# Bringing the score maxima of a group into the queries' tile by two DMAs through memory instead of by TensorE and VectorE

## The chip, the cores and the metric

One core of one Trainium2 chip. The metric is the device time of one execution in microseconds (us). All times here are of that one core.

## What is computed

The input is x, 16 sequences ("quarters", q = 0 to 15) of 512 tokens with 256 features. Six residual blocks follow each other; the code names them by letters:

```python
x = x + 0.5 * _L0_ffn_ref(_layernorm(x), ...)     # A: coupling network, 3 cycles
x = x + _L0_attn_ref(_layernorm(x), ...)          # B: causal attention, 16 heads, latent keys, rope
x = x + 0.5 * _L0_ffn_ref(_layernorm(x), ...)     # C
x = x + 0.5 * _L1_ffn_ref(_layernorm(x), ...)     # D: small feature network
x = x + _L1_attn_ref(_layernorm(x), ...)          # E: attention with strided keys, then an MLP (E2)
x = x + 0.5 * _L1_ffn_ref(_layernorm(x), ...)     # F
```

What matters here is the softmax inside B and E:

```python
scores = jnp.einsum('bhqd,bhkd->bhqk', q, k) * scale
attn = jax.nn.softmax(scores, axis=-1)
```

Everything is float32. A row maximum is taken from the scores before the exponential.

## The kernel before

All weights stay in SBUF. The kernel is a software pipeline over the 16 sequences: `TURN` (L30) is a list of steps written out by hand, such as `1:max.B.1.2`, "for the sequence one turn ahead, stage B, group 1, round 2 of the maxima". `all_steps` (L101) unrolls it over the turns t; every engine walks the same list and runs its own part of each step, so each engine's queue is in this order and semaphores join them. Some 16 turns of about 215 us are in full swing, with a shorter opening and ending.

Attention works by groups of four heads (`GROUPS` = 4); head j of a group has the 32 partitions from 32j on, of which 16 hold the head's features. There are 4 groups for B and 4 for E in each sequence, 128 in all. A group goes through these steps:

- `content` (and `turn`, the rope part of B): queries and keys into tiles of `MAT`, and a copy in a faster format into `HI` by GpSimd.
- `max` (`maxima`, L636, on TensorE; `row_maxima`, L896, on VectorE): scores with the queries on the partitions, from `HI`, and their row maxima into `MX` (L208), which has the queries of one tile on the 128 partitions.
- `shift`: TensorE transposes `MX` (four 128x128 transposes, `turned`, L486, called at L784), so that the maxima lie along a row again, and `shifted` (L918) on VectorE subtracts the result from the whole queries' tile in `MAT`. `MX` is zero but in columns 16, 48, 80 and 112, so that only row 16 of each head's 32 rows changes: minus the maximum of each query. The keys' tile holds 1.0 in that row (`c_one`, through the bias at L1135, and through `c_qkb` for E, L1017), so that the product of queries and keys is the score less its maximum.
- `exp` (`exponents`, L665): the scores again, transposed and from `MAT`, one to four rounds for a group; round 0 begins with a wait for the shift (L668). ScalarE takes the exponentials into `PR` (L1174).
- `sum`, `divide`: the values weighted and divided.

In PSUM, banks 0 to 3 are used in pairs (`max`, `exp` and two more), bank 4 holds the sums, and banks 5 to 7 go round for all else, the shift included. TensorE works in order: when `exp` waits, all that stands behind it in the list waits too.

Round 0 of B's `exp` stands close behind the group's last `max` in the list: for group 0, between `max.B.0.2` and `exp.B.0.0` are `tf.C.1`, `divide.E.0`, `content.B.1`, `v.B`, `shift.B.0`, `att.E` and `mix.C.1`.

SyncE (SP) issues all DMAs. After the weights it walks over the sequences (L1361 to L1375): it waits until the last block F of a sequence has been added to `X`, stores it, waits until the store has landed and loads another sequence into the same place.

Of the kernel before, what the change touches and what calls it, by code (L numbers as in the profile page):

```python
# [7 lines left out]
F32 = mybir.dt.float32  # L8
# [6 lines left out]
P = 128  # L15
# [8 lines left out]
HALVES_OVER = [(n + RD // 2) % RD for n in range(RD)]  # L24
LN_EPS = 1e-5
# [6 lines left out]
0:mix.C.2.1 1:exp.B.0.2 -1:up.1 1:turn.B.2.q 1:max.B.1.2 -1:up.2 1:content.B.2 0:back.C -1:up.3 1:shift.B.1 -1:up.4  # L32
0:stats.D 1:exp.B.1.0 0:normal.D -1:up.5 -1:up.6 1:max.B.2.0 -1:bias.E2.0 0:xt.D -1:up.7 1:max.B.2.1 0:inner.D
0:relu.D.0 -1:down.0 1:max.B.2.2 -1:bias.E2.1 0:relu.D.1 0:relu.D.2 0:relu.D.3 0:bias.D.0 -1:down.1 1:sum.B.0.2
0:bias.D.1 -1:centre 1:exp.B.1.1 1:shift.B.2 1:sum.B.1.0 -1:scale 1:exp.B.1.2 -1:stats.F 1:sum.B.1.1 1:turn.B.3.k
-1:normal.F 1:exp.B.2.0 0:mout.D -1:xt.F -1:bias.F.0 0:stats.E 1:turn.B.3.q -1:inner.F -1:relu.F.0 1:divide.B.0
0:normal.E -1:relu.F.1 1:content.B.3 -1:relu.F.2 1:sum.B.1.2 -1:bias.F.1 1:exp.B.2.1 1:sum.B.2.0 -1:relu.F.3
1:exp.B.2.2 0:xt.E 1:max.B.3.0 0:content.E.3 0:bias.E.0 -1:mout.F 1:max.B.3.1 0:part.E.0 1:sum.B.2.1 1:max.B.3.2
0:part.E.1 1:divide.B.1 0:v.E 1:shift.B.3 0:max.E.3.0 1:sum.B.2.2 2:stats.A 2:normal.A 1:exp.B.3.0 0:content.E.2
1:exp.B.3.1 1:sum.B.3.0 2:xt.A 1:divide.B.2 1:exp.B.3.2 2:h1.A.0 0:content.E.1 2:h2.A.0 0:shift.E.3 0:max.E.2.0  # L40
2:h3.A.0 1:sum.B.3.1 1:sum.B.3.2 0:shift.E.2 2:tf.A.0 0:max.E.1.0 2:mix.A.0.0 0:content.E.0 0:bias.E.1 2:mix.A.0.1
2:h1.A.1 1:divide.B.3 0:max.E.1.1 2:h2.A.1 1:att.B 2:h3.A.1 0:exp.E.3.0 2:tf.A.1 2:mix.A.1.0 1:proj.B 2:mix.A.1.1
0:exp.E.2.0 1:stats.C 2:h1.A.2 0:sum.E.3.0 1:normal.C 2:h2.A.2 0:shift.E.1 1:xt.C 2:h3.A.2 0:max.E.0.0 0:divide.E.3
2:tf.A.2 2:mix.A.2.0 0:sum.E.2.0 2:mix.A.2.1 0:max.E.0.1 1:h1.C.0 2:back.A 0:exp.E.1.0 2:stats.B 0:divide.E.2
2:normal.B 1:h2.C.0 0:max.E.0.2 0:sum.E.1.0 1:h3.C.0 2:xt.B 1:tf.C.0 0:max.E.0.3 2:latent.B 0:shift.E.0 1:mix.C.0.0
0:exp.E.1.1 2:turn.B.0.k 0:exp.E.0.0 0:sum.E.1.1 2:kvt.B 2:turn.B.0.q 0:exp.E.0.1 0:sum.E.0.0 2:content.B.0
0:exp.E.0.2 0:exp.E.0.3 0:sum.E.0.1 1:mix.C.0.1 2:turn.B.1.k 1:h1.C.1 2:max.B.0.0 2:turn.B.1.q 1:h2.C.1 0:divide.E.1
2:max.B.0.1 0:sum.E.0.2 0:sum.E.0.3 1:h3.C.1 2:max.B.0.2 1:tf.C.1 0:divide.E.0 2:content.B.1 2:v.B 2:shift.B.0
# [66 lines left out]
def build(nc, ins, out):  # L115
# [14 lines left out]
    with ctx:  # L130
# [51 lines left out]
        c_one, c_ones = col(), col(4)  # L182
# [25 lines left out]
        MX = sb("MX", [P, TT, P])  # L208
# [107 lines left out]
        with nc.Block() as block:  # L316
# [81 lines left out]
            def _(pool):  # L398
# [5 lines left out]
                pool.affine_select(out=c_ones, in_=c_ones, compare_op=ALU.not_equal, fill=1.0, base=-HD,  # L404
# [43 lines left out]
        with nc.Block() as block:  # L448

            @block.tensor  # L450
            def _(pe):
# [297 lines left out]
                for name, *a in STEPS:  # L749
# [64 lines left out]
            def _(dve):  # L814
# [211 lines left out]
                for name, *a in STEPS:  # L1026
# [20 lines left out]
                    elif name == "shift":  # L1047
                        shifted(*a)
# [364 lines left out]
```

## Time and profile before

| | us |
|---|---|
| median of 3 runs | 3690.88 |
| lowest and highest | 3689.16, 3691.62 |
| span of the profiled execution, first to last instruction | 3688.1 |

The page of the profile gives the span of the profiled execution and no total of its own; the median of the runs is 2.8 us above that span. Of the span, TensorE's matmuls are busy 3457.0 us (94%), VectorE 2271.7 us (62%), ScalarE 1887.2 us (51%), GpSimd 955.1 us (26%). The program moves data over its DMA queues almost only in the first 50 us; afterwards there is one store and one load of 512 KB in each turn.

How to read it: PE is TensorE, PEld its weight loads, DVE VectorE, ACT ScalarE, POOL GpSimd, SP SyncE; SPq marks instructions by which SP issues a DMA. A row of the timeline has start in us, duration in us, engine, line, operation, output <- input, and xN, the number of instructions that it merges.

### The profile page before, as it was taken

How to read it: one execution, taken by the hardware profiler on the slowest of the kernel's cores; microseconds unless marked ns; L12 is line 12 of the kernel's file. 1: busy time of each engine (PE TensorE's matmuls, PEld its weight loads, DVE VectorE, ACT ScalarE, POOL GpSimd, SP SyncE). 2: the span in 40 equal slices, each digit the busy share in tenths (PEclk: the TensorE clock that was granted, in tenths of full speed). 3: DMA queues.
4: the chain of work that ended last, by engine and by line, in shares of the span. 5: the costliest groups of instructions: out<-in, count | busy, mean ns of one | idle time of the engine just before them, and what ended most of it. 6: DMA issues, size and time to landing. Idle time of an engine off the chain costs nothing.

```text
span 3688.1 us, 63212 instructions
## 1 busy us (share of the span) xinstructions
PE 3457.0 (94%) x24928; PEld 2002.6 (54%) x24928; DVE 2271.7 (62%) x4778; ACT 1887.2 (51%) x2919; POOL 955.1 (26%) x1069
## 2 busy tenths in 40 slices
PE   4789999999999999999999999999999999999876
PEld 3355556565555656555555655555565555555443
DVE  3446576666756666675666667566666756676442
ACT  2234655546465564646556464555646555564422
POOL 2213132331313232131222323122231313223111
PEclk8798999999999999999999999999999999999977
DMA  3000000000000000000000000000000000000000
GB/s 92 1 1 1 1 1 12 1 13 1 13 1 1 13 1 13 1 13 1 1 12 1 13 1 8 5 1 13 1 13 1 1 13 1 12 1 7 1 6 6
DMA packets 40882, 27.73 MB, mean 8 GB/s; under 512 B 19600, under 2 KB 39696, under 8 KB 40592
## 3 DMA queue, kind: packets, MB, share of 16 engines
q1 hardware_dynamic: 40592, 23.69, 2.2%
q8 instruction: 203, 3.33, 0.4%
q14 instruction: 87, 0.71, 0.1%
HBM read 15.30 MB, written 8.39 MB: 6 GB/s over the span
## 4 chain that ended last, share of the span: by engine, by line
PE 82%; DVE 12%; ACT 3%; issue 2%; POOL 0%; DVEq 0%; ACTq 0%; POOLq 0%
PE ps L478 74%; PE ps L489 8%; DVE MX L915 2%; DVE XN L843 1%; ACT other L1200 1%; DVE MX L909 1%; DVE XN L894 1%; DVE XN L891 1%; DVE XT L854 1%; DVE LT L881 1%; DVE XN L892 1%; DVE XT L853 1%; ACT PR L1174 0%; DVE stats L834 0%; DVE other L851 0%
## 5 line engine op out<-in xcount | busy, mean ns | idle before, releaser
L1174 ACT ACTIVATE PR<-ps 128x1024 f32<-128x1024 f32 (+3 forms) x592 | 524.5, 931 | 341.9 <-PE ps L478 340.6
L478 PE MATMUL ps<-MAT 32*128 32x512 f32 (+5 forms) x4928 | 593.3, 503 | 14.4 <-DVE MX L909 4.4
L915 DVE TENSOR_REDUCE MX<-ps 128x2 f32<-128x1024 f32 (+3 forms) x512 | 391.8, 818 | 203.7 <-PE ps L478 201.4
L1246 POOL TENSOR_TENSOR rstd<-var,neg_half 128x4 f32<-128x4 f32 x144 | 148.7, 1033 | 1311.3 <-DVE var L826 1183.5
L478 PEld LDWEIGHTS ps<-MAT 32*128 32x128 f32 (+2 forms) x4928 | 290.4, 199 | 262.4 <-issue 162.7
L478 PE MATMUL ps<-XT,cn_w 128*128 128x256 f32 x1536 | 367.6, 390 | 13.5 <-DVE XT L853 8.5
L478 PEld LDWEIGHTS ps<-XT,cn_w 128*128 128x128 f32 x1536 | 290.5, 193 | 99.7 <-issue 28.7
L478 PE MATMUL ps<-other,cn_w 128*128 128x512 f32 (+2 forms) x1152 | 321.0, 480 | 16.1 <-ACT other L1082 5.4
L921 DVE SCALAR_TENSOR_TENSOR MAT<-ps,MAT 128x512 f32<-128x512 f32 x128 | 88.5, 691 | 300.9 <-PE ps L489 300.3
L1281 POOL TENSOR_TENSOR MAT<-XN 128x512 f32<-128x512 f32 x128 | 167.3, 1307 | 402.4 <-DVE XN L894 241.8
L1304 POOL TENSOR_SCALAR_AFFINE_SELECT PR<-PR 128x512 f32<-128x512 f32 (+1 forms) x192 | 158.8, 827 | 410.0 <-ACT PR L1174 409.8
L909 DVE TENSOR_REDUCE MX<-ps 128x2 f32<-128x1024 f32 (+6 forms) x256 | 220.0, 902 | 59.6 <-PE ps L478 58.8
L1295 POOL CAST HI<-MAT 128x512 fp32r<-128x512 f32 (+3 forms) x256 | 146.4, 585 | 388.2 <-ACT MAT L1141 248.4
L478 PE MATMUL ps<-XT,w_up 128*128 128x512 f32 x512 | 245.7, 611 | 0.9 <-ACT XT L1073 0.9
L478 PE MATMUL ps<-HI 32*128 32x256 f32 (+4 forms) x3072 | 209.2, 360 | 36.4 <-DVE MX L915 25.4
L1082 ACT ACTIVATE other<-ps,cols 128x512 f32<-128x512 f32 x192 | 121.4, 683 | 228.3 <-PE ps L478 228.3
L478 PE MATMUL ps<-w_down,other 128*128 128x256 f32 x1024 | 227.4, 380 | 0.0
L843 DVE TENSOR_SCALAR XN<-X,mv,rstd 128x256 f32<-128x256 f32 x384 | 183.6, 540 | 67.6 <-POOL rstd L1246 67.0
L1200 ACT ACTIVATE other<-ps,cols 128x512 f32<-128x512 f32 x256 | 179.2, 795 | 71.4 <-PE ps L478 71.4
L478 PEld LDWEIGHTS ps<-HI 32*128 32x128 f32 x3072 | 117.3, 192 | 176.3 <-issue 136.5
L478 PEld LDWEIGHTS ps<-w_down,other 128*128 128x128 f32 x1024 | 193.4, 190 | 33.9 <-issue 7.7
L1183 ACT ACTIVATE AO<-ps 128x512 f32<-128x512 f32 x128 | 77.0, 602 | 255.5 <-PE ps L478 255.3
(158 smaller groups left out, 5718.2 us busy)
## 6 DMA issues: line engine op xcount, KB each, us to landing
X<-in_L_attn_x SPq DMA_DIRECT2D x16, 512.0 KB, 3.9
out<-X SPq DMA_DIRECT2D x16, 512.0 KB, 3.0
w_up<-in_L_attn_W SPq DMA_DIRECT2D x1, 1024.0 KB, 6.8
w_down<-in_L_attn_W SPq DMA_DIRECT2D x1, 1024.0 KB, 8.8
w_krope<-in_L_attn_W_krope SPq DMA_DIRECT2D x1, 512.0 KB, 4.4
w_qk<-in_L_attn_Wqkv SPq DMA_DIRECT2D x4, 128.0 KB, 4.4
cn_w<-in_L_ffn_cn_w SPq DMA_DIRECT2D x1, 256.0 KB, 4.2
w_qrope<-in_L_attn_W_qrope SPq DMA_DIRECT2D x1, 256.0 KB, 3.1
```

The source lines that it names most:

```text
L478: return pe.matmul(dst, lhsT, rhs, start=start, stop=stop, skip_group_check=True)
L489: last = pe.transpose(dst[:, t * P:(t + 1) * P], src(t), ident[:])
L843: last = dve.tensor_scalar(XN[:, c, t, :], src[:, t, :], mv[:, c, t, 0:1], rstd[:, c, t:t + 1], ALU.subtract, ALU.mult)
L909: last = dve.tensor_reduce(MX[:, t0:t0 + len(parts), at], src[:, :, 0:len(parts) * nk].rearrange("p j (t k) -> p t j k", k=nk), AX_X, ALU.max)
L915: last = dve.tensor_reduce(MX[:, t, at], src[:, :, a:a + nk[pair]], AX_X, ALU.max)
L1082: freed(act.activation(H1[:, area_of[s], m, :], src, ACT.Gelu, bias=c_b1[:, m:m + 1]), "h1", s, q, k, m)
L1174: freed(act.activation(PR[0:m, tile_of((s, q, g, r)), 2 * pair:2 * pair + 2, lo:T], ps[0:m, b:b + 2, 0:T - lo], ACT.Exp, scale=SCALE[s]), ...
L1200: last = act.activation(U[:, area_of[s], j, :], src, ACT.Relu, scale=c_mw1[:, j:j + 1], bias=c_mb1[:, j:j + 1])
L1246: pool.tensor_tensor(rstd[:, c, :], var[:, c, :], neg_half[:], ALU.pow).then_inc(rstd_ready.sem, 1)
L1281: pool.tensor_tensor(dst, a, b, ALU.add).then_inc(rope_sum.sem, 1)
L1295: pool.tensor_copy(HI[:, content_tile((s, q, g), w, hi=True), 0:n], MAT[:, content_tile((s, q, g), w), 0:n]).then_inc(hi_ready.sem, 1)
L1304: pool.affine_select(out=p, in_=p, compare_op=ALU.is_ge, fill=0.0, base=0, pattern=[[0, 4], [0, n], [1, P]], channel_multiplier=-1).then_i ...
```

## The change

`shift` is no longer a step of the list: all `shift` tokens are taken out of `TURN`, and the order of all others stays. `MX` becomes four buffers (`SHIFTS` = 4) of 4 heads x 4 tiles for each partition, and needs no zeros around it. As soon as VectorE is through with the last `max` of a group, SP writes the 128 x 16 maxima to a scratch tensor in memory, element by element in the transposed order (each element is 4 bytes, and neighbours in the source lie 512 bytes apart in the destination), waits until they have landed, and reads them back as four rows of 512 into partitions 16, 48, 80 and 112 of the queries' tile in `MAT`. The row now holds plus the maximum, and the keys' row -1.0 in place of 1.0 (`c_less`). Round 0 of `exp` waits for the landing of the second transfer. SP's loop over the sequences is put into the order of the list, with the transfers among the stores and loads.

```diff
+SHIFTS = 4
-        MX = sb("MX", [P, TT, P])
+        MX = sb("MX", [P, SHIFTS, 4, TT])
+        maxima_d = nc.dram_tensor("maxima_d", (SHIFTS, 4, T), F32, kind="Internal").ap()
...
                 def exponents(s, q, g, r):
                     if r == 0:
-                        read_out(pe, "shift", s, q, g)
+                        n = number[s, q, g]
+                        pe.wait_ge(shift_landed[n % SHIFTS], 16 * (n // SHIFTS + 1))
...
-                    elif name == "shift":
-                        read_out(pe, *last_max(*a))
-                        turned(single_bank(), ("shift", *a), lambda t: MX[:, t, :])
...
                 def row_maxima(s, q, g, m):
-                    if m == 0 and n:
-                        when_full(dve, "shift", *GROUPS_DONE[n - 1])
+                    if m == 0 and n >= SHIFTS:
+                        dve.wait_ge(shift_landed[n % SHIFTS], 16 * (n // SHIFTS))
...
-                def shifted(s, q, g):
-                    src = when_full(dve, "shift", s, q, g)
-                    queries = MAT[:, content_tile((s, q, g), "q"), :]
-                    freed(dve.scalar_tensor_tensor(queries, src, -1.0, queries, ALU.mult, ALU.add), "shift", s, q, g)
...
+                def shifted(s, q, g):
+                    n = number[s, q, g]
+                    read_out(sp, *last_max(s, q, g))
+                    row, at = HD, n % SHIFTS
+                    sp.dma_start(maxima_d[at].rearrange("j (t p) -> p (j t)", p=P), MX[:, at, :, :],
+                                 allow_slow_non_contiguous=True).then_inc(maxima_out[at], 16)
+                    sp.wait_ge(maxima_out[at], 16 * (n // SHIFTS + 1))
+                    sp.dma_start(MAT[row:P:ROWS, content_tile((s, q, g), "q"), :], maxima_d[at]).then_inc(shift_landed[at], 16)
+
+                loaded_next(2)
+                for name, *a in STEPS:
+                    if name == "mout" and a[0] == "F":
+                        stored(a[1])
+                    elif name == "max" and a[3] == last_max(*a[0:3])[4]:
+                        shifted(*a[0:3])
```

## Rows read from the trace of the kernel before

**Rows 1.** The page: busy time, granted clock in 40 slices, chain.

```profile
PE 3457.0 (94%) x24928; PEld 2002.6 (54%) x24928; DVE 2271.7 (62%) x4778; ACT 1887.2 (51%) x2919; POOL 955.1 (26%) x1069
...
PEclk8798999999999999999999999999999999999977
...
PE 82%; DVE 12%; ACT 3%; issue 2%; POOL 0%; DVEq 0%; ACTq 0%; POOLq 0%
```

**Rows 2.** Groups by form: busy us, mean ns, idle before, of the shift.

```profile
L921 DVE SCALAR_TENSOR_TENSOR MAT<-ps,MAT 128x512 f32<-128x512 f32 x128 | 88.5, 691 | 300.9 <-PE ps L489 300.3
...
L489 PE MATMUL ps<-ident,MX 128*128 128x128 f32 x512 | 84.4, 290 | 7.7 <-DVE MX L909 6.4 <-DVE MX L915 1.2
```

**Rows 3.** Timeline, B's group 0: DVE's last maxima, then PE's shift to exp.

```profile
1549.30 1.95 DVE L915 TENSOR_REDUCE MX<-ps 128x2 f32<-128x256 f32 x4 [1.19 <-PE ps L478]
...
1553.08 0.66 PE L489 MATMUL ps<-ident,MX 128*128 128x128 f32 x4
1553.57 1.04 PE L489 MATMUL ps<-ident,ATN 128*128 128x128 f32 x8
1554.59 2.02 PE L478 MATMUL ps<-MAT 32*128 32x512 f32 x16
```

**Rows 4.** Timeline, last maxima and first exp of E0, B1, B2, B3.

```profile
1516.10 1.82 DVE L909 TENSOR_REDUCE MX<-ps 128x2 f32<-128x1024 f32 x2 [1.12 <-PE ps L478]
1523.10 1.26 PE L478 MATMUL ps<-MAT 32*128 32x512 f32 x8
...
1582.91 1.94 DVE L915 TENSOR_REDUCE MX<-ps 128x2 f32<-128x256 f32 x4
1590.14 2.01 PE L478 MATMUL ps<-MAT 32*128 32x512 f32 x16
...
1610.51 1.93 DVE L915 TENSOR_REDUCE MX<-ps 128x2 f32<-128x256 f32 x4
1625.58 2.01 PE L478 MATMUL ps<-MAT 32*128 32x512 f32 x16
...
1654.56 1.95 DVE L915 TENSOR_REDUCE MX<-ps 128x2 f32<-128x256 f32 x4 [1.68 <-PE ps L478]
1660.24 2.92 PE L478 MATMUL ps<-MAT 32*128 32x512 f32 x16
```

**Rows 5.** DMA issues: output<-input, count, KB each, median us to landing.

```profile
w_qdec<-in_L_attn_W_qdec SPq DMA_DIRECT2D x1, 128.0 KB, 4.4
...
cols<-in_L_attn_b SPq DMA_DIRECT2D x1, 4.0 KB, 2.4
...
cols<-in_L_ffn_W SPq DMA_DIRECT2D x4, 2.0 KB, 2.3
...
cols<-in_L_attn_beta SPq DMA_DIRECT2D x1, 1.0 KB, 2.1
...
rows<-in_L_attn_bout SPq DMA_DIRECT2D x1, 128.0 KB, 8.7
```

**Rows 6.** Timeline, VectorE's last addition of F and SP's store and load.

```profile
1649.69 1.28 DVE L967 TENSOR_TENSOR X<-ps,X 128x512 f32<-128x512 f32 x2
...
1651.04 0.38 SPq L1366 DMA_DIRECT2D out<-X  x1
1654.71 0.37 SPq L1368 DMA_DIRECT2D X<-in_L_attn_x  x1
```

**Rows 7.** Timeline of PE: an idle time in full swing; one product, opening and later.

```profile
1526.92 0.44 PE L570 MATMUL ps<-ident,LT 128*128 128x128 f32 x2 [1.59 <-DVE LT L881]
...
49.97 5.93 PE L478 MATMUL ps<-XT,cn_w 128*128 128x256 f32 x16 [2.66 <-DVE XT L853]
...
1560.09 3.62 PE L478 MATMUL ps<-XT,cn_w 128*128 128x256 f32 x16
```

**Rows 8.** Windows: length, busy times (x), then granted clock, DMA share, GB/s.

```profile
47.60:54.50 6.90, 4.54 (x11) 3.64 (x12) 2.95 (x8) 1.55 (x4) 0.00 (x0) 0.51 0.84 131
...
1658.70:1662.10 3.40, 3.40 (x32) 1.46 (x32) 3.21 (x12) 0.60 (x1) 0.04 (x1) 0.50 0.00 0
1662.10:1873.80 211.70, 207.01 (x1521) 120.57 (x1514) 138.43 (x285) 117.28 (x179) 58.85 (x65) 1.00 0.02 5
```

More of the change, by code:

```diff
@@ L31 @@
 1:turn.B.2.k 0:h2.C.2 -1:xt.E2 1:max.B.1.0 0:h3.C.2 1:sum.B.0.0 1:sum.B.0.1 0:tf.C.2 1:max.B.1.1 0:mix.C.2.0 -1:up.0
[L32 to L45, printed above, removed]
@@ L46 @@
-0:exp.E.1.1 2:turn.B.0.k 0:exp.E.0.0 0:sum.E.1.1 2:kvt.B 2:turn.B.0.q 0:exp.E.0.1 0:sum.E.0.0 2:content.B.0
-0:exp.E.0.2 0:exp.E.0.3 0:sum.E.0.1 1:mix.C.0.1 2:turn.B.1.k 1:h1.C.1 2:max.B.0.0 2:turn.B.1.q 1:h2.C.1 0:divide.E.1
-2:max.B.0.1 0:sum.E.0.2 0:sum.E.0.3 1:h3.C.1 2:max.B.0.2 1:tf.C.1 0:divide.E.0 2:content.B.1 2:v.B 2:shift.B.0
+0:mix.C.2.1 1:exp.B.0.2 -1:up.1 1:turn.B.2.q 1:max.B.1.2 -1:up.2 1:content.B.2 0:back.C -1:up.3 -1:up.4 0:stats.D
+1:exp.B.1.0 0:normal.D -1:up.5 -1:up.6 1:max.B.2.0 -1:bias.E2.0 0:xt.D -1:up.7 1:max.B.2.1 0:inner.D 0:relu.D.0
@@ new lines @@
+-1:down.0 1:max.B.2.2 -1:bias.E2.1 0:relu.D.1 0:relu.D.2 0:relu.D.3 0:bias.D.0 -1:down.1 1:sum.B.0.2 0:bias.D.1
+-1:centre 1:exp.B.1.1 1:sum.B.1.0 -1:scale 1:exp.B.1.2 -1:stats.F 1:sum.B.1.1 1:turn.B.3.k -1:normal.F 1:exp.B.2.0
+0:mout.D -1:xt.F -1:bias.F.0 0:stats.E 1:turn.B.3.q -1:inner.F -1:relu.F.0 1:divide.B.0 0:normal.E -1:relu.F.1
+1:content.B.3 -1:relu.F.2 1:sum.B.1.2 -1:bias.F.1 1:exp.B.2.1 1:sum.B.2.0 -1:relu.F.3 1:exp.B.2.2 0:xt.E 1:max.B.3.0
+0:content.E.3 0:bias.E.0 -1:mout.F 1:max.B.3.1 0:part.E.0 1:sum.B.2.1 1:max.B.3.2 0:part.E.1 1:divide.B.1 0:v.E
@@ new lines @@
+0:max.E.3.0 1:sum.B.2.2 2:stats.A 2:normal.A 1:exp.B.3.0 0:content.E.2 1:exp.B.3.1 1:sum.B.3.0 2:xt.A 1:divide.B.2
+1:exp.B.3.2 2:h1.A.0 0:content.E.1 2:h2.A.0 0:max.E.2.0 2:h3.A.0 1:sum.B.3.1 1:sum.B.3.2 2:tf.A.0 0:max.E.1.0
+2:mix.A.0.0 0:content.E.0 0:bias.E.1 2:mix.A.0.1 2:h1.A.1 1:divide.B.3 0:max.E.1.1 2:h2.A.1 1:att.B 2:h3.A.1
+0:exp.E.3.0 2:tf.A.1 2:mix.A.1.0 1:proj.B 2:mix.A.1.1 0:exp.E.2.0 1:stats.C 2:h1.A.2 0:sum.E.3.0 1:normal.C 2:h2.A.2
+1:xt.C 2:h3.A.2 0:max.E.0.0 0:divide.E.3 2:tf.A.2 2:mix.A.2.0 0:sum.E.2.0 2:mix.A.2.1 0:max.E.0.1 1:h1.C.0 2:back.A
@@ L49 @@
+0:exp.E.1.0 2:stats.B 0:divide.E.2 2:normal.B 1:h2.C.0 0:max.E.0.2 0:sum.E.1.0 1:h3.C.0 2:xt.B 1:tf.C.0 0:max.E.0.3
+2:latent.B 1:mix.C.0.0 0:exp.E.1.1 2:turn.B.0.k 0:exp.E.0.0 0:sum.E.1.1 2:kvt.B 2:turn.B.0.q 0:exp.E.0.1 0:sum.E.0.0
+2:content.B.0 0:exp.E.0.2 0:exp.E.0.3 0:sum.E.0.1 1:mix.C.0.1 2:turn.B.1.k 1:h1.C.1 2:max.B.0.0 2:turn.B.1.q 1:h2.C.1
+0:divide.E.1 2:max.B.0.1 0:sum.E.0.2 0:sum.E.0.3 1:h3.C.1 2:max.B.0.2 1:tf.C.1 0:divide.E.0 2:content.B.1 2:v.B
 0:att.E 1:mix.C.1.0 1:mix.C.1.1 2:exp.B.0.0 0:proj.E 0:stats.E2 1:h1.C.2 0:normal.E2 2:exp.B.0.1
@@ L224, in build @@
         const_pool, const_dve = sem("const_pool"), sem("const_dve")
-        PREPARED_FIRST, PREPARED_ALL, POOL_DONE = 14, 22, 25
+        PREPARED_FIRST, PREPARED_ALL, POOL_DONE = 14, 22, 24
         x_loaded = [sem(f"x_loaded{c}") for c in range(CH)]
         x_stored = [sem(f"x_stored{c}") for c in range(CH)]
+        shift_landed = [sem(f"shift_landed{n}") for n in range(SHIFTS)]
+        maxima_out = [sem(f"maxima_out{n}") for n in range(SHIFTS)]
+        maxima_d = nc.dram_tensor("maxima_d", (SHIFTS, 4, T), F32, kind="Internal").ap()
         full = [sem(f"bank_full{b}") for b in range(8)]
@@ L1360, in _, with loaded_next, stored @@
                     sp.dma_start(dst, src, allow_slow_non_contiguous=True).then_inc(loaded, 16)
-                for q in range(2, N):
-                    c = q % CH
-                    if q >= CH:
-                        for n in range(2):
-                            read_out(sp, "mout", "F", q - CH, n)
-                        sp.dma_start(o_v[q - CH], X[:, c]).then_inc(x_stored[c], 16)
-                        sp.wait_ge(x_stored[c], 16 * (q // CH))
-                    sp.dma_start(X[:, c], x_v[q]).then_inc(x_loaded[c], 16)
-                for q in range(N - CH, N):
+                def loaded_next(q):
+                    sp.dma_start(X[:, q % CH], x_v[q]).then_inc(x_loaded[q % CH], 16)
+                def stored(q):
                     c = q % CH
```

24 lines of the change are left out of this document (12 added, 12 removed).

## The prediction

> **What bounds the kernel now.** I read the page first: its busy times, the granted clock by slices and the chain that ended last. TensorE is busy 94% of the span, the slices in the middle hold their clock, and the chain is TensorE for 82% [rows 1]. The windows say it more sharply: in one turn in full swing TensorE is busy 207.0 of 211.7 us at the full clock [rows 8]. So the kernel is a queue of TensorE work. What is taken from that queue is gained; VectorE (62%) and ScalarE (51%) have room. And what makes the queue wait is lost nearly whole, since there are only some 4.7 us of idle time in a turn into which a wait could fall.
>
> Next I read the groups by form for what is removed [rows 2], then, for the one new wait, the timeline around the last maxima of each kind of group and its first `exp` [rows 3, 4]. The reader should look there at one number: the time from the end of VectorE's last reduction to TensorE's first product from `MAT`. That is the time in which the two transfers must be done. The DMA issues with their landings [rows 5] and SP's own queue [rows 6] price the transfers.
>
> **What is removed.** The subtraction: 128 x 0.691 us = 88.5 us of VectorE [rows 2]. It isn't what TensorE's queue waits for most of the time, so I count nothing for it; what hides it is VectorE's own idle time, and the wait of `exp` for it is replaced below. The transposes: 512 on TensorE. One lasts 290 ns in the mean, but they are pipelined; four of them hold the queue from 1553.08 to 1553.57, 0.5 us [rows 3]. There are 8 groups in a turn and 16 sequences: 128 x 0.5 = **64 us gained**. That is the whole gain that I can point to. Banks 5 to 7 are asked for once less in a group; no wait in the rows read hangs on them, so zero, with a few us either way in the range.
>
> **What is added: the path of the maxima.** After VectorE's last reduction of a group the path is: SP sees the semaphore; it issues the write of 2048 single elements; these land; SP issues the read back; that lands; TensorE goes on. No row shows such a transfer, so I go by the nearest.
> - SP's reaction: VectorE ends at 1650.97 and SP's store stands at 1651.04 [rows 6], 0.07 us; twice, 0.15 us.
> - The write. From below, `cols` of 4.0 KB is 1024 pieces of 4 bytes and landed 2.4 us after its issue; from above, the slowest 128 KB of the trace landed after 8.7 us [rows 5], though it waited behind two loads of 1 MB. Nearest in the number of pieces is `w_qdec`: 128 partitions with 16 runs each are 2048 pieces, of 64 bytes; it landed after 4.4 us [rows 5]. I take **4.4 us**, since the number of pieces, not their bytes, is what the two have in common. It may be less (it stood behind other small pieces) or more (all these rows write to SBUF and mine writes 4-byte pieces to memory).
> - The read back: four rows of 2 KB. Small loads land after 2.1 to 2.4 us [rows 5]; I take 2.3.
>
> Sum: 4.4 + 2.3 + 0.15 = 6.85, say **7.0 us** with the last semaphore; 4.85 from below (2.4 + 2.3 + 0.15), 11.25 from above (8.7 + 2.4 + 0.15).
>
> The Trainium skill (page "DMA: Bandwidth & Descriptors", section "Anatomy of one DMA") gives a DMA about 2.0 us fixed plus its bytes over 436 GB/s, measured for another issuing path. The rows agree with the fixed part for small loads (2.1 us) and not for 128 KB in 2048 pieces (4.4 us). By that rule the estimate for the two would be some 4.2 us, and the time that of the first rival below. The same page ("Rules for kernel authors") speaks against the change: a strided last dimension becomes one descriptor for each element, and a transpose by a rearranged access pattern is to be avoided. No run here shows such a write yet; that rule stands beside the second rival.
>
> **How much time the path has now.** From the end of the last reduction to the first `exp`:
> - B0: 1551.25 to 1554.59, 3.3 us [rows 3].
> - E0: 1517.92 to 1523.10, 5.2 us; B1: 1584.85 to 1590.14, 5.3 us; B3: 1656.51 to 1660.24, 3.7 us [rows 4].
> - B2: 1612.44 to 1625.58, 13.1 us [rows 4]; E1, E2 and E3, read in the same way, have more than that. These four are hidden at any price up to 13 us.
>
> Without the transposes that lie in it, each of these is 0.5 us shorter. The new idle time of TensorE is 7.0 less what is left: B0 4.2, B1 2.2, B3 3.8, E0 2.3. Together 12.5 us in a turn, x 16 = **200 us lost**. What is queued behind the waiting `exp` is everything: projections, coupling networks, the MLP. ScalarE, VectorE and GpSimd run dry with it, and none can give work back since TensorE is the bound.
>
> One wait that is there now goes away in exchange: behind E0's first `exp` TensorE is idle for 1.59 us at 1526.92 until VectorE has scaled `LT` [rows 7]; VectorE gets there without the `exp`, so a stop of 2.3 us just before it swallows it: 1.6 x 16 = **26 us back**.
>
> **The clock.** TensorE's clock doesn't come through long waits. In the opening, an idle time of 2.66 us goes with half clock (0.51 in that window [rows 8], the lower of the two levels, 1.2 GHz), and the 16 products behind it took 5.93 us where they take 3.62 us at the full clock [rows 7]: 2.3 us more. In full swing the idle time of 1.59 us goes without a loss. The clock has little to spare even now: it falls once in the turn, for 3.4 us, with TensorE busy all the time but on products of 32 rows [rows 8], and B3's first `exp` took 2.92 us there where B1's took 2.01 [rows 4]. So for B0 and B3 (4 us idle) I count 2.3 us each, for B1 and E0 (2.2 us, between the two cases) half of it: 2 x 2.3 + 2 x 1.15 = 6.9 us in a turn, x 16 = **110 us lost**.
>
> **SP's queue.** Each group puts two issues and a wait of 4 to 5 us on SP. SP also has the store and the load of a sequence; at 1651.04 it stores and at 1654.71 it loads [rows 6], and B3's maxima come at 1656.51, after both, so SP is free. The load has a queue in common with the maxima and may hold them up for a part of its flight; at most 2 us in 13 turns, 26 us, in the range only. E3's maxima come 3.5 us after B3's and wait for SP some 1 us, covered by over 30 us. VectorE's new wait before it writes `MX` is for the group four before and long fulfilled.
>
> **Sum.** -64 + 200 - 26 + 110 = +220 us. Span 3688.1 + 220 = 3908; the 2.8 us between span and median added, **3910 us**, 6% slower.
>
> **Rivals.**
> 1. *Both transfers at the smallest landing: faster.* 2.1 + 2.1 + 0.15 = 4.35 us. Then B0 waits 1.5 us and B3 1.1 us, the others not, no wait is long enough for the clock, and 2.6 x 16 = 42 us stand against the 64: 3669 us. For it: every small load lands so soon, and 8 KB is small [rows 5]. Against it: 2048 pieces, and the one row with as many took 4.4. It decides from below about 4.8 us for the path; at 4.85 without a loss of clock the sum is 3686 us, no change. 12 in 100: 7 faster, 5 the same.
> 2. *Scattered 4-byte writes are slow.* The path takes 11.25 us: waits of 8.4, 6.5, 8.0 and 6.6 us, less the 1.6, are 27.9 x 16 = 446; the clock falls four times in a turn, 4 x 2.3 x 16 = 147; with the 64 gained, +529: 4220 us. For it: no row has a write of small pieces to memory. Against it: in the rows pieces cost little. 20 in 100, of which a third beyond 4220.
> 3. *The waits as forecast, but the clock holds.* +110: 3801 us. For it: in full swing TensorE is busy before and behind each stop, unlike in the opening. Against it: the clock falls now without any stop. 18 in 100.
> 4. The forecast, with a path of 5.5 to 9 us and a loss of clock: 50 in 100.
>
> **How the numbers follow.** The forecast's own bounds are the path from 5.5 to 9 us. The range has to leave out no more than 2 in 10: from below the path at 4.85 us, with the half charge of the clock for B0 and B3 (-64 + 59 + 37 = +32), 3723, rounded to 3720; above, rival 2 at 4220. Left out are most of rival 1 and the slowest third of rival 2. A measurement of this kernel tells about 0.2%, 7 us, from no change. Slower by more than that holds in rivals 2 and 3 and the forecast, 0.88; faster 0.07; the same 0.05.
>
> **What would show it.** In the profile after: landings for the two new issues (4.4 and 2.3 us); TensorE idle before the first `MAT` product of B0 and B3 by about 4 us, of B1 and E0 by about 2 us, and of the other four by nothing; TensorE's busy time in a turn down by 4 us; slices of the granted clock below full in the middle of the run, with falls behind B0's and B3's stops; the idle time before `LT` gone. I'm wrong if the write lands under 2.5 us, if it lands over 8, or if the clock stays up.

## The result and the profile after

The changed kernel takes 4282.9 us in the median where the one before takes 3690.65 in the same comparison: a ratio of 1.160 (95% interval 1.1585 to 1.1618), 16% slower. The direction was forecast, the size was not: 3910 us was predicted, and the time lies above the range (3720 to 4220).

From the page of the profile after, the lines that answer to [rows 1]: busy times, granted clock in 40 slices, and the chain that ended last, by engine and by line.

```profile
span 4279.2 us, 62140 instructions
...
PE 3518.6 (82%) x24416; PEld 1984.2 (46%) x24416; DVE 2207.9 (52%) x4650; ACT 1886.1 (44%) x2919; POOL 964.8 (23%) x1068
...
PEclk8788999989989998999899999989999998999877
...
PE 63%; DMA 19%; DVE 13%; ACT 3%; issue 2%; POOL 0%; DVEq 0%; ACTq 0%; SPq 0%; POOLq 0%
PE ps L481 58%; DMA maxima_d<-MX 16%; PE ps L492 4%; DVE MX L916 4%; DMA MAT<-maxima_d 3%; DVE MX L910 1%; DVE XN L844 1%; ACT other L1194 1%; DVE XN L895 1%; DVE XN L892 1%; DVE XT L855 1%; DVE XN L893 1%; DVE XT L854 1%; DVE stats L835 0%; DVE other L852 0%
```

Three things stand in these lines. The DMAs, absent from the chain before, are 19% of it, and 16 of the 19 are the write of the maxima, 3 the read back. TensorE works less of the time (82% for 94%) but is busy 62 us longer, although 512 transposes are gone. And the slices of the granted clock that were full all through the middle now have 8s among them.

The DMA issues (KB each, median us from issue to landing; the landing of the last line is not given) and, from the list of waits (total us, times, longest), those of TensorE for the transfer and for `LT`:

```profile
maxima_d<-MX SPq DMA_DIRECT2D x128, 8.0 KB, 10.3
MAT<-maxima_d SPq DMA_DIRECT2D x128, 8.0 KB
...
PE ps L481 <- DMA MAT<-maxima_d: 559.4, 69, 12.6
...
PE ps L573 <- DVE LT L882: 7.4, 2, 3.7
```

The write lands after **10.3 us**; the prediction had 4.4. The timeline at B's group 0 of one turn shows the whole path; it answers to [rows 3]. VectorE's last maxima, SP's two issues, TensorE before and behind its wait:

```profile
2063.18 1.95 DVE L916 TENSOR_REDUCE MX<-ps 128x2 f32<-128x256 f32 x4 [1.19 <-PE ps L481]
...
2065.16 0.36 SPq L1369 DMA_DIRECT2D maxima_d<-MX  x1
2075.16 0.50 SPq L1372 DMA_DIRECT2D MAT<-maxima_d  x1
...
2066.95 1.09 PE L492 MATMUL ps<-ident,ATN 128*128 128x128 f32 x8
2077.02 3.81 PE L481 MATMUL ps<-MAT 32*128 32x512 f32 x16 [8.97 <-DMA MAT<-maxima_d]
```

The reduction ends at 2065.13; SP answers 0.03 us later, issues the read back 10.0 us after the write, and TensorE goes on 1.9 us after that: 11.9 us for a path that had 3.3. TensorE stands still for 8.97 us, and the 16 products behind the wait take 3.81 us where the same 16 took 2.02 in [rows 3].

The same turn has three more such waits, of E0, B1 and B3:

```profile
2036.95 2.11 PE L481 MATMUL ps<-MAT 32*128 32x512 f32 x8 [7.05 <-DMA MAT<-maxima_d]
...
2121.30 3.81 PE L481 MATMUL ps<-MAT 32*128 32x512 f32 x16 [6.89 <-DMA MAT<-maxima_d]
...
2202.70 3.81 PE L481 MATMUL ps<-MAT 32*128 32x512 f32 x16 [9.10 <-DMA MAT<-maxima_d]
```

Together with B0 that is 32.0 us in the turn. B2, E1, E2 and E3 wait for nothing there, as forecast.

Windows over B0's transfer (columns as in [rows 8]; the last three are granted clock, DMA share, GB/s) show what the chip did in that time:

```profile
2065.20:2068.50 3.30, 2.85 (x21) 1.93 (x20) 3.20 (x8) 3.13 (x5) 2.05 (x4) 1.00 0.31 7
2068.50:2071.00 2.50, 0.00 (x0) 0.00 (x0) 0.99 (x3) 2.03 (x3) 0.00 (x0) 1.00 0.00 0
2071.50:2076.00 4.50, 0.00 (x0) 0.00 (x0) 0.00 (x0) 0.00 (x0) 0.00 (x0) 0.50 0.00 0
2077.00:2081.50 4.50, 4.48 (x18) 1.92 (x19) 0.00 (x0) 0.65 (x1) 0.00 (x0) 0.50 0.00 0
```

The DMA engines have records of work only in the first 3.3 us after the issue of the write; the other 6.7 us until the landing pass with a DMA share of 0.00. And the granted clock falls to half while TensorE stands still, and is still at half when its products start again.

### The profile page after: what moved, and what is told of

Its sections match the earlier page's. It is cut to its first block, busy times and chain, and to the rows that moved or that the text cites. A ratio compares the mean times of both kernels' runs of the same rounds, so it can differ in the third digit from the quotient of the medians.

```text
span 4279.2 us, 62140 instructions
## 1 busy us (share of the span) xinstructions
PE 3518.6 (82%) x24416; PEld 1984.2 (46%) x24416; DVE 2207.9 (52%) x4650; ACT 1886.1 (44%) x2919; POOL 964.8 (23%) x1068
## 4 chain that ended last, share of the span: by engine, by line
PE 63%; DMA 19%; DVE 13%; ACT 3%; issue 2%; POOL 0%; DVEq 0%; ACTq 0%; SPq 0%; POOLq 0%
PE ps L481 58%; DMA maxima_d<-MX 16%; PE ps L492 4%; DVE MX L916 4%; DMA MAT<-maxima_d 3%; DVE MX L910 1%; DVE XN L844 1%; ACT other L1194 1%; DVE XN L895 1%; DVE XN L892 1%; DVE XT L855 1%; DVE XN L893 1%; DVE XT L854 1%; DVE stats L835 0%; DVE other L852 0%
## 5 line engine op out<-in xcount | busy, mean ns | idle before, releaser
L481 PE MATMUL ps<-MAT 32*128 32x512 f32 (+5 forms) x4928 | 676.0, 577 | 569.7 <-DMA MAT<-maxima_d 559.4
L481 PEld LDWEIGHTS ps<-MAT 32*128 32x128 f32 (+2 forms) x4928 | 308.8, 217 | 859.1 <-DMA MAT<-maxima_d 618.5
L892 DVE TENSOR_TENSOR XN<-ps,rope_sin 128x512 f32<-128x512 f32 x128 | 88.3, 690 | 330.4 <-PE ps L481 330.4
L921 DVE RECIPROCAL rden<-ps 128x16 f32<-128x16 f32 x128 | 32.3, 252 | 337.4 <-PE ps L492 336.9
## 6 DMA issues: line engine op xcount, KB each, us to landing
maxima_d<-MX SPq DMA_DIRECT2D x128, 8.0 KB, 10.3
```

The source lines that it names most:

```text
L481: return pe.matmul(dst, lhsT, rhs, start=start, stop=stop, skip_group_check=True)
L892: dve.tensor_tensor(b, src, rope_sin[:], ALU.mult).then_inc(rope_sines.sem, 1)
```

## The experiments

The waits of TensorE, the landings of the transfers and the clock were measured on kernels in which the way of the maxima differs. First the write. In most of these kernels the read back changes with it, so the landing of the write (the median of the 128 transfers of one execution) is what counts; their total times are of a single execution each. The later kernels, those with a ratio, ran four or five times.

### A contiguous write, the transposition moved to the read

```diff
-        maxima_d = nc.dram_tensor("maxima_d", (SHIFTS, 4, T), F32, kind="Internal").ap()
+        maxima_d = nc.dram_tensor("maxima_d", (SHIFTS, P, 4 * TT), F32, kind="Internal").ap()
-  sp.dma_start(maxima_d[at].rearrange("j (t p) -> p (j t)", p=P), MX[:, at, :, :], ...)
+  sp.dma_start(maxima_d[at], MX[:, at, :, :].rearrange("p j t -> p (j t)"))
-  sp.dma_start(MAT[row:P:ROWS, ..., :], maxima_d[at])
+  sp.dma_start(MAT[row:P:ROWS, ..., :].rearrange("j (t p) -> j t p", p=P), maxima_d[at].rearrange("p (j t) -> j t p", j=4), ...)
```

> The scratch tensor is laid out as the maxima lie in SBUF, so the write is 128 pieces of 64 bytes and the read back gathers 2048 pieces of 4 bytes; same values, the transposition only moves from the write to the read. In the changed kernel the write landed 10.3 us after its issue and the read back let TensorE go on 1.9 us after its own. Theory 1 (writing 2048 pieces of 4 bytes into memory is what is slow; reading as many is not): the write lands after 2.1 to 2.5 us; the read, on four destination rows, after 2 to 6 us; path 4.5 to 8.5 us, time 3720 to 4040 us. Theory 2 (2048 pieces are slow in whichever direction): write 2.3, read about 10 us, path 12.3, time about 4280 us as now. Theory 3 (any write of maxima to memory takes 10 us until it is confirmed): write stays at about 10 us, time 4280 us or more.

Measured: 3991.8 us, beside 3696.9 for the kernel before. The write's landing, and the same group of the timeline:

```profile
maxima_d<-MX SPq DMA_DIRECT2D x128, 8.0 KB, 1.4
...
1917.57 1.95 DVE L916 TENSOR_REDUCE MX<-ps 128x2 f32<-128x256 f32 x4 [1.20 <-PE ps L481]
...
1919.55 0.32 SPq L1369 DMA_DIRECT2D maxima_d<-MX  x1
1920.95 0.52 SPq L1371 DMA_DIRECT2D MAT<-maxima_d  x1
...
1928.10 2.96 PE L481 MATMUL ps<-MAT 32*128 32x512 f32 x11 [5.66 <-DMA MAT<-maxima_d]
```

A write of 128 pieces lands after 1.4 us, less than any load of [rows 5]; theory 3 is out. The read of 2048 pieces of 4 bytes, into four partitions, takes 7.2 us here until TensorE goes on (6.9 in the median of the groups that wait): dearer than theory 1 allowed, cheaper than theory 2 said. The path is 8.6 us in place of 11.9, and 290 us of the loss are gone. So scattering the write costs 8.9 us more than writing straight (10.3 less 1.4), and gathering the read some 5 us more than reading straight (6.9 less 1.9).

### Pieces of 16 bytes

The scratch tensor is laid out as heads x queries of a tile x tiles; the write has 512 pieces, of which four share 64 bytes, and the read goes by four transfers.

```diff
+        maxima_d = nc.dram_tensor("maxima_d", (SHIFTS, 4, P, TT), F32, kind="Internal").ap()
+  sp.dma_start(maxima_d[at].rearrange("j p t -> p j t"), MX[:, at, :, :], ...)
+  for j in range(4):
+      sp.dma_start(<row j of MAT>, maxima_d[at, j:j + 1].rearrange("o p t -> o t p"), ...)
```

> The scratch tensor as heads x queries of a tile x tiles: the write is 512 pieces of 16 bytes in place of 2048 of 4 bytes, the read back gathers pieces of 4 bytes by four transfers, one a head. Theory 1a (each small piece costs its time at the memory): the landing of the write falls in proportion to the pieces, 2.3 + 8.0 x (512 - 128)/(2048 - 128) = 3.9 us. Theory 1b (a fixed wait until scattered writes are confirmed, whatever their number): it stays near 10 us. The read back then takes 2.5 to 4 us; with 1a the path is 6.5 to 8 us and the time 3850 to 4000 us.

Measured: the write lands after 2.7 us, even sooner than in proportion to the pieces (3.9). A fixed wait for scattered writes (theory 1b) is out. The whole was no faster, 4312.7 us, and far from the 3850 to 4000 expected: the four gathering reads took what the write gave, with 593 us of waits of TensorE in all. In one group SP needs 6.05 us only to issue them, and in the median TensorE goes on 10.1 us after the first issue, not 2.5 to 4.

```profile
maxima_d<-MX SPq DMA_DIRECT2D x128, 8.0 KB, 2.7
...
2004.06 6.05 SPq L1374 DMA_DIRECT2D MAT<-maxima_d  x4
...
PE ps L481 <- DMA MAT<-maxima_d: 593.3, 74, 12.5
```

### As many pieces, but each with 64 bytes of its own

```diff
+        maxima_d = nc.dram_tensor("maxima_d", (SHIFTS, 4, T, 16), F32, kind="Internal").ap()
+  sp.dma_start(maxima_d[at, :, :, 0].rearrange("j (t p) -> p j t", p=P), MX[:, at, :, :], ...)
```

> Again 2048 pieces of 4 bytes into memory, but each into 64 bytes of its own (the scratch tensor is 16 times as large; read back with the same stride), so that no two writes fall into the same 64 bytes. Theory 1a (cost by the number of pieces): the write lands after about 10.3 us as before. Theory 1c (writes that share 64 bytes, 16 of them here, wait for one another): it lands after at most 4.5 us. The read back tells what gathering 2048 pieces costs, 2 to 6 us; time with 1a 4250 to 4450 us, with 1c 3850 to 4050 us.

Measured: 4195.1 us, and the write, still 2048 pieces of 4 bytes, lands after 4.3 us:

```profile
maxima_d<-MX SPq DMA_DIRECT2D x128, 8.0 KB, 4.3
```

That is the landing of theory 1c, and nearly the 4.4 us that the prediction took from `w_qdec`. 2048 pieces were priced rightly in size. What the price left out is that in the changed kernel 16 of them fall into the same 64 bytes. The time was expected at 3850 to 4050 us and came out higher, since the read back, which now gathers too, takes 6.8 us in the median until TensorE goes on (2 to 6 expected).

### The same scatter, into SBUF

```diff
+        SC = sb("SC", [P, 16, 16])
+  sp.dma_start(SC[:, :, 0], MX[:, at, :, :].rearrange("p j t -> p (j t)"), ...).then_inc(scattered, 16)
+  sp.wait_ge(scattered, 16 * (n + 1))
   sp.dma_start(maxima_d[at], MX[:, at, :, :].rearrange("p j t -> p (j t)"))
```

> As the kernel with the contiguous write, with one more transfer ahead of the others in each group, which SP waits for: the same 2048 pieces of 4 bytes from MX into a scratch tile of SBUF, 64 bytes apart. It prices the scatter by itself with another destination. Theory 1 (the memory as destination is what makes the pieces slow): the scatter lands after 2.5 to 4.4 us. Rival (2048 pieces of 4 bytes cost 10 us into any destination): about 10 us.

Measured: 2048 pieces of 4 bytes from SBUF to SBUF, 64 bytes apart, land after 2.9 us. The landing is in the range of theory 1, but with 4.3 us for the like pieces in memory, the memory as destination is dearer by 1.4 us only; it doesn't explain the 10.3. The nearness of 4.3 to the 4.4 of `w_qdec`, whose destination was SBUF, is thus in part chance. The time was 4212.7 us, since each group paid for one more transfer.

```profile
SC<-MX SPq DMA_DIRECT2D x128, 8.0 KB, 2.9
```

### What the sharing depends on

The kernel with 64 bytes for each piece also had a scratch region 16 times as large. Five layouts part the two; all write the same 2048 pieces, and each (called by its label, e8 to e15, below) differs from the kernel with the contiguous write in the scratch tensor's last two dimensions.

```diff
+  e8:  maxima_d (SHIFTS, P, 16, 2),    pieces at [..., 0:16, 0]:   8 bytes apart, partitions 128 bytes
+  e9:  maxima_d (SHIFTS, P, 128, 2),   pieces at [..., 0:16, 0]:   8 bytes apart, partitions 1024 bytes
+  e15: maxima_d (SHIFTS, P, 136, 2),   pieces at [..., 0:16, 0]:   8 bytes apart, partitions 1088 bytes
+  e14: maxima_d (SHIFTS, P, 16, 8),    pieces at [..., 0:16, 0]:  32 bytes apart, partitions 512 bytes
+  e13: maxima_d (SHIFTS, P, 16, 16),   pieces at [..., 0:16, 0]:  64 bytes apart, partitions 1024 bytes
```

> As the kernel with the contiguous write, but every element of the scratch tensor has 8 bytes, so that the write is again 2048 pieces of 4 bytes. Here 8 pieces share 64 bytes, as 16 do in the changed kernel, but all 8 come from one partition and so from one DMA engine, one after another. With 64 bytes for each piece the write landed after 4.3 us, with 16 pieces from 16 partitions in the same 64 bytes after 10.3. If any sharing of 64 bytes is what costs, the write lands after 6 us or more; if only pieces that come from several partitions hinder each other, after 2.5 to 4.5 us. The read back is as with the contiguous write, 6.8 us; time 4100 to 4300 us, not what this run is for.

> As the kernel whose pieces of one partition stand 8 bytes apart (8 pieces in the same 64 bytes, landing 9.9 us), but the partitions now lie 1 KB apart in memory, so that the 2048 pieces spread over 128 KB, as in the kernel with 64 bytes for each piece (landing 4.3 us). It parts the two things that differed between those: the sharing of 64 bytes, and the size of the region. If sharing 64 bytes is the cause, the write still lands after 9 to 10 us; if writing so many pieces into a region of 8 or 16 KB is the cause, it lands after 4 to 5 us. The read back is as before, 6.8 us.

> The partitions lie 1 KB apart in memory as in the kernel that took 18.9 us, but each of the 16 pieces of a partition has 64 bytes of its own. If the sharing of 64 bytes is the cause and the distance of 1 KB only makes it worse, the write lands after 4 to 5 us; if the distance of 1 KB by itself is slow, after 15 us or more.

> Pieces 32 bytes apart, two in the same 64 bytes, partitions 512 bytes apart. Own 64 bytes gave 4.3 us, 8 in the same 9.9. If the unit that is shared has 64 bytes and each sharing costs: 5 to 7 us. If the unit has 32 bytes: 4.3 us as with no sharing. If the distance between partitions decides: between 10 and 19 us.

> As the kernel that took 18.9 us (8 pieces in the same 64 bytes, partitions 1 KB apart), with 1088 bytes from partition to partition in place of 1024. If the doubling from 9.9 to 18.9 us comes from the distance being a power of two, the write lands after about 10 us again; if it comes from the spread over a larger region, it stays near 19 us.

The landings of the write, a line from the DMA issues of each kernel, in the order e8, e9, e13, e14, e15:

```profile
maxima_d<-MX SPq DMA_DIRECT2D x128, 8.0 KB, 9.9
```

```profile
maxima_d<-MX SPq DMA_DIRECT2D x128, 8.0 KB, 18.9
```

```profile
maxima_d<-MX SPq DMA_DIRECT2D x128, 8.0 KB, 5.1
```

```profile
maxima_d<-MX SPq DMA_DIRECT2D x128, 8.0 KB, 6.6
```

```profile
maxima_d<-MX SPq DMA_DIRECT2D x128, 8.0 KB, 10.7
```

| pieces in the same 64 bytes | distance of the partitions, bytes | landing, us |
|---|---|---|
| 1 (e3) | 64 | 4.3 |
| 1 (e13) | 1024 | 5.1 |
| 2 (e14) | 512 | 6.6 |
| 8, of one partition (e8) | 128 | 9.9 |
| 8, of one partition (e15) | 1088 | 10.7 |
| 8, of one partition (e9) | 1024 | 18.9 |
| 16, of 16 partitions (the change) | 4 | 10.3 |

Sharing is the cause that all rows agree on: with the distance held at 1024 bytes, own 64 bytes give 5.1 and shared ones 18.9. (The pieces of 16 bytes fit in: 512 of them, four to 64 bytes, 2.7.) That 64 bytes is the unit that counts isn't settled by these rows: pieces 32 bytes apart are still dearer (6.6), but no run has them 128 bytes or more apart. It matters little whether the pieces that share come from one partition or from 16. For e8, e13, e14 and e15 the landings are what sharing as the cause led to expect (9.9 us for 6 or more, 5.1 for 4 to 5, 6.6 for 5 to 7, 10.7 for about 10).

The expectation for e9 failed: 9 to 10 us were expected and 18.9 came. Sharing and a distance of 1024 bytes together cost twice as much as sharing alone, and 64 bytes more of distance take that away (e15), so the larger region is not to blame; for the changed kernel this second effect is without meaning.

Why shared writes land late isn't shown by any run: the landings say when, not what the memory does. In the changed kernel, in e8 and in e9 alike the records of the DMA engines end within 3.4 us of the issue (DMA share 0.28 to 0.31 until then, 0.00 behind it), and with own 64 bytes (e3) the share in that stretch is the same 0.28; so the added time lies behind the work that is on record. The kernel e8 was expected at 4100 to 4300 us; its path is 9.9 us and 7.2 for the read, 17.1 in all, more than the 13 us that B2 has, and TensorE waits 956 us. The times of these kernels (4664.4, 5647.1, 4262.1, 4373.1 and 4766.6 us for e8, e9, e13, e14 and e15) follow the landing and the gathering read.

### Only the groups that have time

Groups B2, E1, E2 and E3 as in the change, the other four with TensorE's transposes and an addition by VectorE.

```diff
+DIRECT = (("B", 2), ("E", 3), ("E", 2), ("E", 1))
+        by_dma = {e: n for n, e in enumerate(e for e in GROUPS_DONE if (e[0], e[2]) in DIRECT)}
...
+  if (s, q, g) in by_dma: pe.wait_ge(shift_landed[...], ...)
+  else: read_out(pe, "shift", s, q, g)
```

> The two slow transfers as in the changed kernel, but only for groups B2, E1, E2 and E3, which have 13 us or more; B0, B1, B3 and E0 keep the transposes on TensorE (and an addition in place of the subtraction, since the keys' row is now -1). If the loss is only the waits of the four groups with little time, this is faster than before: 64 transposed groups fewer x 0.5 us = 32 us, about 3659 us, ratio 0.991; the transfers still take 12 us each and cost nothing. Rival (the transfers cost by their traffic or by holding up SP's loads, wherever they stand): 3700 us or more.

Measured: 3673.4 us, ratio 0.996 (0.9943 to 0.9975). The same two slow transfers, 64 times over, and the kernel is a little faster than before. So neither their traffic nor SP's queue costs anything that shows; the loss of the change is the waits of the four groups that have 3 to 5 us, and the slower products behind them. But 17 us came in where 32 were expected. The two profiles divide the difference: TensorE is busy 3433.2 us, 24 less than before, where 32 were expected, and 11.6 us go into waits for transfers that arrive late in the opening and the ending, where even these groups have less time.

```profile
PE ps L486 <- DMA MAT<-maxima_d: 11.6, 6, 5.2
```

### The shift left out, and the transposes doubled

These two price what the change removes. In the first, neither transposes nor subtraction nor transfer are there, and no maximum is subtracted.

```diff
-                        read_out(pe, "shift", s, q, g)
+                        read_out(pe, *last_max(s, q, g))
...
-                        turned(single_bank(), ("shift", *a), lambda t: MX[:, t, :])
...
-                        shifted(*a)
```

> The kernel before with the shift left out: neither transposes nor subtraction nor any transfer, the exponentials are taken of scores from which no maximum is subtracted. It is the most that any way of hiding the shift can give. By the prediction's term (128 x 0.5 us of TensorE): 3691 - 64 = 3627 us, ratio 0.983. Rival, from the kernels in which the waits are gone and half clock lasts longer than before (298 against 257 us): without these dense products of 128 rows the clock falls oftener, and 40 to 50 us remain: 3641 to 3651 us, ratio 0.987 to 0.989.

Measured: 3623.6 us, ratio 0.981 (0.9796 to 0.9829), 69 us faster: the 64 us of the prediction and a little more. This is the most that hiding the shift can bring. Beside the profile before, TensorE is busy 52.5 us less (3457.0 less 3404.5) and idle 13.1 us less (231.1 less 218.0): the four transposes of a group are worth 0.41 us, and the rest of the gain is waits that go with them.

```profile
span 3622.5 us, 61805 instructions
...
PE 3404.5 (94%) x24416; PEld 1958.8 (54%) x24416; DVE 2208.6 (61%) x4650; ACT 1885.1 (52%) x2919; POOL 963.3 (27%) x1069
...
PEclk8799999999999999999999999999999999999977
```

The rival, that the clock suffers when these products are gone, is refuted here: the middle holds its clock.

```diff
-                        turned(single_bank(), ("shift", *a), lambda t: MX[:, t, :])
+                        for n in range(2 * TT):
+                            last = pe.transpose(dst[:, n % TT * P:(n % TT + 1) * P], MX[:, n % TT, :], ident[:])
```

> The kernel before with each of the 512 transposes of the maxima done twice, the second over the first; nothing else differs. By the prediction's price (0.5 us for four) it is 64 us slower: 3755 us, ratio 1.017. If the clock profits from these products, as the rival of the kernel without a shift has it, less: 3730 to 3745 us.

Measured: 3736.1 us, ratio 1.012 (1.0101 to 1.0131): 43 us for 512 transposes more, not 64. That is in the range named for a clock that profits (3730 to 3745), and the mean granted clock was 0.968 to 0.970 in its four runs, 0.964 to 0.968 in those of the kernel before; but leaving the transposes out did not lower it. One price doesn't hold in both directions: a group's four transposes cost 0.34 us when doubled and give 0.54 when they go with the subtraction and its waits, 0.41 of it in products. What part the clock has in the 0.34 stays open.

### A path without sharing: VectorE turns the blocks first

`MX` is 32 columns wide for each group, VectorE transposes its 32x32 blocks (0.2 us), four transfers write 64 pieces of 128 bytes into the rows of the changed kernel, and the contiguous read stays.

```diff
+                        dve.transpose(MXT[:, n % SHIFTS, :], MXW[:, n % SHIFTS, :]).then_inc(maxima_turned, 1)
...
+                    for b in range(P // ROWS):
+                        sp.dma_start(maxima_d[at, :, ROWS * b:ROWS * (b + 1)], MXT[ROWS * b:ROWS * b + 4 * TT, at, :])...
```

> All eight groups without TensorE, but VectorE turns the 32x32 blocks of the maxima first, so that the write is 64 pieces of 128 bytes, by four transfers, into the same rows from which the contiguous read takes them. Path: 0.3 us for the transposition and its wait, 3 x 0.38 us for the issues ahead, 1.4 to 1.6 until the last has landed, 1.9 for the read back: 4.7 to 5.0 us in place of 12.2. With the rule that a group waits for the path less its time plus 0.5 us: B0 2.2, B1 0.2, B3 1.8, E0 0.3 us in a turn, 4.5 x 16 = 72 us, less 64 for the transposes, less the idle time before LT that E0's wait covers (5), plus 20 to 60 for the clock: 3710 to 3750 us. If the rule is wrong and every DMA costs as much as in the changed kernel: over 4000 us.

Measured: 3754.5 us, ratio 1.018 (1.016 to 1.0206), just above what was expected (3710 to 3750); TensorE's waits for the transfers are 104 us where 72 were expected. One group, VectorE's last maxima, SP's issues and TensorE:

```profile
1798.72 1.96 DVE L919 TENSOR_REDUCE MXW<-ps 128x2 f32<-128x256 f32 x4 [1.20 <-PE ps L484]
...
1801.02 1.69 SPq L1378 DMA_DIRECT2D maxima_d<-MXT  x4
1804.25 0.49 SPq L1381 DMA_DIRECT2D MAT<-maxima_d  x1
...
1806.16 2.10 PE L484 MATMUL ps<-MAT 32*128 32x512 f32 x8 [2.58 <-DMA MAT<-maxima_d]
...
PE ps L484 <- DMA MAT<-maxima_d: 104.1, 49, 5.9
```

Nothing of the computation is left out, and of the 592 us of loss 528 are gone by writing 64 runs of 128 bytes in place of 2048 elements that share 64 bytes (ratios 1.160 and 1.018). What is left is a path of 5 to 5.5 us (5.5 in this group, from 1800.68 to 1806.16) against 3.3 and 3.7.

### Two exp steps later in the list

```diff
-1:exp.B.3.0 0:content.E.2
+0:content.E.2 1:exp.B.3.0
-2:exp.B.0.0 0:proj.E
+0:proj.E 2:exp.B.0.0
```

> As the kernel with VectorE's transposition, and two steps change places in the list: B3's first exp goes behind content.E.2 (2.9 us of products), B0's behind proj.E (3.7 us). The path of 5 us then fits: B3 waits no more, B0 neither, but proj.E may wait about 1 us for ScalarE's copy of att. Then the 64 us of the transposes come in: 3690 - 64 + 16 x 1.2 = 3645 us, ratio 0.988. Rival (the moved steps only shift the wait to ScalarE's exponentials and sums): 3690 to 3720 us.

Measured: 3703.2 us, ratio 1.0045 (1.0027 to 1.0063). The waits for the transfers fell from 104 to 27 us, but the time is that of the rival. Its waits of TensorE:

```profile
PE ps L484 <- DMA MAT<-maxima_d: 27.1, 15, 5.5
PE ps L484 <- ACT PR L1175: 25.3, 24, 2.1
...
PE ps L484 <- ACT ATT L1195: 20.3, 16, 1.3
```

The 16 waits of 1.3 us for `att` were expected; those for ScalarE's exponentials (8.7 us in the kernel without the changed places) are the rival's. Both are moved steps that meet another engine too early: these two moves save 77 us in waits for the transfers and bring 35 us more of waits for ScalarE, and the 3645 us that were expected are not reached.

### The transfers where they fit

> The version to beat both: the path of 5 us (VectorE turns the blocks, four writes, one contiguous read) for the groups that have at least 5 us, that is all but B0 and B3 (and B1 of the first two sequences and E0 of the last two, where less time is there); the others keep TensorE's transposes. 92 of 128 groups lose their 0.5 us: 46 us; less 10 to 15 us for the clock and a few for waits just missed: 3655 to 3665 us, ratio 0.990 to 0.993. Rival (the gain is lost again, as in the kernel with only the hidden groups, by half): 3670 us or more.

```diff
+        by_pe = [(s, q, g) for s, q, g in GROUPS_DONE
+                 if (s, g) in (("B", 0), ("B", 3)) or (s, g) == ("B", 1) and q < 2 or (s, g) == ("E", 0) and q >= N - 2]
```

Measured: 3652.6 us, ratio 0.9895 (0.988 to 0.991), **faster than both**, by 39 of the 69 us that are to be had, and a little better than expected (3655 to 3665). TensorE waits for the transfers 3.7 us in all:

```profile
PE ps L489 <- DMA MAT<-maxima_d: 3.7, 13, 0.9
```

## Why the prediction was wrong

**What bounds the kernel: right.** TensorE's queue decides, and what makes it wait is lost nearly whole.

**The 64 us gained: right in size.** The kernel without a shift gains 69. In part that is luck: 52.5 us of it are TensorE's products (0.41 us for a group, not 0.5), and 13 us are idle time that the prediction put at nothing.

**The path of the maxima: wrong, and this is the step that failed: the landing of the write.** SP's reaction (0.03 us for 0.07) and the read back (1.9 for 2.3) were priced well. The write was put at 4.4 us, after the row with the same number of pieces, and landed after 10.3, beyond even the bound of 8.7. The number of pieces was not the whole of the price: 2048 pieces with 64 bytes each for themselves land after 4.3 us, sharing 64 bytes by 8 or 16 raises it to some 10. The rows of before could not show that, since every row with small pieces in [rows 5] read from memory and wrote to SBUF. The prediction said so, and took the nearest row for the point all the same. Its bound from above was a large load, chosen by length and not by kind, and it bounded nothing; 11.25 us for the path stood in rival 2, and 12.2 came.

**How long each group waits: right.** The rule was path less time at hand plus 0.5 us. With 12.2 us it gives 9.4, 7.4, 9.0 and 7.5 us for B0, B1, B3 and E0, 33.3 in a turn, 533 in 16. The turn shown above has 8.97, 6.89, 9.10 and 7.05 us, 32.0 together. Measured are 559.4 us for all groups; the opening turns have less time than the full ones and wait up to 12.6 us.

**The idle time before `LT`: right.** 28.8 us in 16 waits before, 7.4 us in 2 after, those of the opening: 21 us back for 26.

**The clock: right in kind, and near in size by luck.** Forecast were 110 us, for two stops at 2.3 us and two at half of that. But all four stops came out at 6.9 us or more, and by the prediction's price that is 147 us, as rival 2 has it. Measured are 114: beside the kernel without a shift, whose span is 3622.5 us with 3404.5 busy, TensorE is busy 3518.6 us for the same products. Over 64 stops that is 1.8 us each, not 2.3; B0's 16 products show just that, 3.81 us for 2.02. For the same reason TensorE's busy time did not go down by 4 us in a turn, as was to be seen, but up by 62 us in all. The rest of the difference is idle time, 760.6 us where 218.0 were, 543 more: nearly all of it the 559.4 us of waits for the transfers, less 20 us of the wait for `LT` (27.3 there, 7.4 here). With the mean granted clocks of 0.965 and 0.895, half clock rules for 258 and 899 us (each twice the missing share of the span). Rival 3, that the clock holds, is out. The row of the opening on which the price rested was a weak one: the clock was at half for nearly all of those 2.66 us already (0.56 in the mean from 47.31 to 49.97), while in the changed kernel it is full up to B0's stop and falls in it.

The Trainium skill (page "TensorE: Matmul & The Clock Gate", section "Part 1: The HAM clock gate") has the clock at half rate unless the engine is kept active; by that rule, the trace agrees: the products behind a wait of 8.97 us took 3.81 us for 2.02, at a granted clock of 0.50.

**SP's queue: right that it costs nothing.** The kernel with only the hidden groups sends the slow transfers and is faster than before.

**Rival 2** was the case that came, in mechanism (scattered writes to memory are slow) and near in time: 4220 us for a path of 11.25. With 12.2 in its place the sum gives 3688 - 64 - 26 + 533 + 147 + 3 = 4281 us, beside 4283 measured; that it meets the time so closely is luck, since the clock was 33 us cheaper and the waits were 26 us longer. It had 20 in 100 and a range cut inside it. It deserved more: it was the one case for which there was no row, and the page "DMA: Bandwidth & Descriptors" of the Trainium skill (section "Rules for kernel authors") warns of a transpose by a rearranged access pattern and of one descriptor for each element; the run agrees, with 10.3 us for the rearranged write against 1.4 for the contiguous one, though one element at a time, each in its own 64 bytes, lands after 4.3. The fixed 2.0 us a DMA that the same page of the Trainium skill gives for another issuing path ("Anatomy of one DMA") does not fit here: contiguous, the write landed after 1.4.

## What to carry to other kernels

A transfer on a path with little time is priced by its destination, by the number of its pieces and by which of them fall into the same 64 bytes of memory, not by its bytes or that number alone; where no row of the trace has that kind of transfer, measure it before relying on it, or give the case without a row the larger chance. Measure for each user of the result how much time lies between the last producer and the first consumer: here a path of 5 or even 12 us costs nothing for half of the groups and nearly its whole excess for the rest, so it pays to move only those that have the time. Turn small blocks on an engine with room first, so that the transfers see runs and not elements.

## What the runs showed of the hardware that was not expected

- 2048 writes of 4 bytes to memory land after 4.3 us with own 64 bytes, 6.6 with two in the same 64 bytes, 9.9 to 10.7 with 8 or 16, and 18.9 with 8 and the partitions exactly 1024 bytes apart (10.7 at 1088).
- A contiguous write of 8 KB from 128 partitions lands after 1.4 us, sooner than every small load of [rows 5].
- Gathering 2048 elements of 4 bytes into four partitions takes some 7 us until TensorE goes on, against 1.9 us for four rows of 2 KB; scattering as many inside SBUF over 128 partitions takes 2.9.
- In the slow writes the DMA engines' records end 3.3 us after the issue; the rest of the 10.3 us (and of the 18.9) passes with a DMA share of 0.00 until the landing.
- 512 more transposes cost 43 us, 512 fewer give 52 us of TensorE's busy time; the mean granted clock was 0.968 to 0.970 with more and 0.964 to 0.965 with none.
